# Inverse square roots by one power operation on GpSimd in place of an integer seed on VectorE and twelve Newton operations on GpSimd

## What is computed

```python
h = _layernorm(x) * (1 + ca) + sa              # root of a variance per token: "new.stats"
x = x + ga * attn_ref(h, guides)               # norms of token differences:   "new.dots"
h = _layernorm(x) * (1 + cb) + sb              #                               "new.again"
x = x + gb * ffn_ref(h, ...)                   # two layers of:
    q = l2norm(q) * qs;  k = l2norm(k) * ksc   # 8 heads, norms of q and k:    "proj.rsqrt"
    x = x + local_attention(rotary(q), rotary(k), v) @ wo
    h = (h - mu) / sqrt(var + 1e-05) * lg + lb #                               "ff.stats"
    x = x + (a * gelu(g)) @ w2 + b2
```

## Time and profile before

| | kernel before |
|---|---|
| median of three runs | 1008.69 us (1006.82 to 1008.88) |
| profiled execution: span | 1004.1 us |
| PE busy | 786.4 us (78%) |
| DVE busy | 698.4 us (70%), 1659 instructions |
| ACT busy | 652.1 us (65%) |
| POOL busy | 545.9 us (54%), 1116 instructions |

### The profile page before, as it was taken

How to read it: one execution, slowest core, us unless ns; L and a number is a source line. 1 busy time by engine, 2 the same in 40 slices (tenths; PEclk the granted TensorE clock), 3 DMA queues, 4 the chain that set the end, 5 groups by cost and what they waited for, 6 DMA issues and landing times.

```text
span 1004.1 us, 21260 instructions
## 1 busy us (share of the span) xinstructions
PE 786.4 (78%) x7119; PEld 556.9 (55%) x7151; DVE 698.4 (70%) x1659; ACT 652.1 (65%) x1539; POOL 545.9 (54%) x1116
## 2 busy tenths in 40 slices
PE   3344678797979797797979788898879787979974
PEld 3223456565656575565656565565656565656642
DVE  4466586494997794485897796494998765676742
ACT  1133474686876694686867685686786766867752
POOL 3146472373876481383786483373876563474601
PEclk9657699999999898999999999999999999999996
DMA  6000000000000000000000000000000000000000
GB/s 198 0 1 0 11 1 12 1 2 1 2 2 2 23 2 25 1 2 2 2 1 2 22 3 22 1 1 2 1 2 1 12 2 11 2 2 1 3 7 15
DMA packets 12298, 10.05 MB, mean 10 GB/s; under 512 B 1040, under 2 KB 11288, under 8 KB 12184
## 3 DMA queue, kind: packets, MB, share of 16 engines
q1 hardware_dynamic: 12184, 8.64, 2.8%
HBM read 6.54 MB, written 2.10 MB: 9 GB/s over the span
## 4 chain that ended last, share of the span: by engine, by line
PE 37%; DVE 21%; ACT 16%; issue 15%; POOL 9%; DMA 1%; POOLq 0%; SPq 0%; ACTq 0%; DVEq 0%
ACT probs L738 7%; PE pair L463 6%; PE dense L600 4%; DVE space L1176 3%; DVE q_norm L1179 3%; PE mixed L494 3%; PE dense L563 3%; POOL h_lo L1263 3%; PE dense L564 3%; PE dense L565 2%; PE dense L678 2%; PE pair L526 2%; DVE space L1174 2%; POOL qk L1288 2%; ACT squares L856 2%
## 5 line engine op out<-in xcount | busy, mean ns | idle before, releaser
L1288 POOL TENSOR_TENSOR qk<-space 128x512 f32<-128x512 f32 x128 | 197.3, 1554 | 28.6 <-DVE q_norm L1179 23.9
L738 ACT ACTIVATE probs<-pair,neg_max 128x128 f32<-128x128 f32 x512 | 138.5, 386 | 19.8 <-DVE neg_max L992 19.5
L1176 DVE TENSOR_TENSOR space<-dense,tables 128x512 f32<-128x512 f32 x128 | 87.3, 682 | 44.0 <-ACT space L860 44.0
L678 PE MATMUL dense<-wq_hi,h_hi 128*128 128x512 f32 x192 | 92.8, 483 | 21.5 <-DVE space L1176 12.2
L1285 POOL TENSOR_TENSOR space<-space,tables 128x512 f32<-128x512 f32 x64 | 84.2, 1316 | 30.9 <-ACT space L860 30.9
L856 ACT ACTIVATE squares<-dense 128x512 f32<-128x512 f32 x128 | 77.4, 605 | 34.0 <-PE dense L680 33.0
L463 PE MATMUL pair<-eye_s,probs 128*128 128x128 f32 x512 | 78.4, 286 | 26.0 <-ACT probs L738 26.0
L992 DVE TENSOR_REDUCE neg_max<-pair 128x4 f32<-128x512 f32 x128 | 82.1, 683 | 17.8 <-PE pair L526 17.6
L1179 DVE TENSOR_REDUCE q_norm<-squares 128x8 f32<-128x512 f32 x128 | 86.4, 675 | 0.0
L1277 POOL TENSOR_TENSOR h_lo<-shifted,h_hi 128x512 fp32r<-128x512 f32 x16 | 20.3, 1266 | 121.2 <-DVE h_hi L1163 121.2
L463 PEld LDWEIGHTS pair<-eye_s,probs 128*128 128x128 f32 x512 | 58.7, 145 | 46.6 <-ACT probs L738 44.0
(11 more groups left out here) (175 smaller groups left out, 1966.1 us busy)
## 6 DMA issues: line engine op xcount, KB each, us to landing
x_in<-n_L_attn_embeddings_dram SPq DMA_DIRECT2D x8, 256.0 KB, 3.2
out_dram<-hn SPq DMA_DIRECT2D x8, 256.0 KB, 2.5
qk<-in_L_ffn_wqkv_dram SPq DMA_DIRECT2D x1, 1536.0 KB, 6.2
qk<-in_L_ffn_w_dram SPq DMA_DIRECT2D x1, 682.0 KB, 7.5
wo_s<-in_L_ffn_wo_dram SPq DMA_DIRECT2D x2, 256.0 KB
o_t<-in_L_wmod_dram SPq DMA_DIRECT2D x1, 384.0 KB, 3.4
probs<-const_rotary_dram SPq DMA_DIRECT2D x1, 256.0 KB, 3.7
band_s<-const_band_dram SPq DMA_DIRECT2D x1, 256.0 KB, 7.8
```

The costliest lines, as they stand in the source:

```text
L678: pe.matmul(to[:, :], h_hi[:, rows], wq_hi[:, layer, cols], start=True, stop=False)
L738: last = act.activation(probs[:, ring, hh, :], banks[m][:, hh * P:(hh + 1) * P], ACT.Exp, bias=neg_max[:, ring, hh:hh + 1], scale=1.0)
L1176: dve.tensor_tensor(turned_s[:, t % 2, m, :].rearrange("p (h a b) -> p h a b", h=HEADS, a=2), halves[:, :, ::-1, :], rot(layer, t, 2 * m + 1),
L1288: pool.tensor_tensor(qk[s][:, t, m * INNER:(m + 1) * INNER], turned_c[:, t % 2, m, :], turned_s[:, t % 2, m, :], ALU.add).then_inc(added, 1)
```

## The change

DVE no longer halves the argument and no longer makes the seed; it writes `power`, which is the argument alone, and signals POOL. POOL raises it to -0.5 in one tensor_tensor with the operation `pow` against a tile `minus_half` that DVE filled with -0.5 at the start. The semaphores of the Newton steps and of DVE's wait on itself go, `root` is no longer written by DVE, and the first `proj.tile` of each pair gets a wait of DVE on `qk_powered`, its own last argument. The order of the steps on every engine stays as it is. The setup's own root of the guides keeps its integer seed and Newton steps on DVE.

```diff
-            def rsqrt_seed(root_, half_, ins_sem):
-                dve.tensor_scalar(root_.bitcast(I32), half_.bitcast(I32), -0.5, RSQRT_SEED, ALU.mult, ALU.add).then_inc(ins_sem, 1)
...
+            dve.memset(minus_half[:, :], -0.5).then_inc(halves_set, 1)
...
-                chain.done(dve.tensor_scalar(half_, mean_var_[:, :, 1], 1e-5, 0.5, ALU.add, ALU.mult))
-                rsqrt_seed(root_, half_, seeded)
+                dve.tensor_scalar(power_, mean_var_[:, :, 1], 1e-5, None, ALU.add).then_inc(powered, 1)
...
-                    own.done(dve.tensor_scalar(half_n[:, :], col[:, SS, :], 1e-30, 0.5, ALU.max, ALU.mult))
-                    rsqrt_seed(root_n[:, :], half_n[:, :], new_seeded)
+                    dve.tensor_scalar(power_n[:, :], col[:, SS, :], 1e-30, None, ALU.max).then_inc(new_powered, 1)
...
+                    if t % 2 == 0 and m == 0 and past(2 * before + t // 2):
+                        dve.wait_ge(qk_powered, 2 * before + t // 2)
                     dve.tensor_reduce(q_norm[:, 16 * (t % 2) + 8 * m:16 * (t % 2) + 8 * m + 8],
...
-                    dve.tensor_scalar(half[:, :], q_norm[:, :], 1e-24, 0.5, ALU.max, ALU.mult).then_inc(qk_self, 1)
-                    dve.wait_ge(qk_self, pair_ + 1)
-                    rsqrt_seed(root[:, :], half[:, :], qk_seeded)
+                    dve.tensor_scalar(power[:, :], q_norm[:, :], 1e-24, None, ALU.max).then_inc(qk_powered, 1)
...
-            def newton(root_, half_, scratch_, threes, base_sem, base, done_sem):
-
-                count = base
-                for k in range(3):
-                    for n, (to, a, b, op) in enumerate(((scratch_, root_, root_, ALU.mult), (scratch_, scratch_, half_, ALU.mult),
-                                                        (scratch_, threes, scratch_, ALU.subtract),
-                                                        (root_, root_, scratch_, ALU.mult))):
-                        ins = pool.tensor_tensor(to, a, b, op)
...
+            pool.wait_ge(halves_set, 1)
+
+            def inverse_root(to, of):
+
+                return pool.tensor_tensor(to, of, minus_half[:, 0:of.shape[-1]], ALU.pow)
 
             def unit_root(pair_):
 
-                pool.wait_ge(qk_seeded, pair_ + 1)
-                newton(root[:, :], half[:, :], scratch[:, :], three_halves[:, :], qk_newton, NEWTON * pair_, qk_rooted)
+                pool.wait_ge(qk_powered, pair_ + 1)
+                inverse_root(root[:, :], power[:, :]).then_inc(qk_rooted, 1)
```

More of the change, by code:

```diff
@@ L52 @@
 RSQRT_SEED = float(0x5F3759DF - (1 << 22))
-NEWTON = 11
 ROW_LN_G, ROW_LN_B, ROW_B2, ROW_B1 = 0, DEPTH, 2 * DEPTH, 3 * DEPTH
@@ L209, in adaln_block @@
         tables = sb("tables", [P, DEPTH, 2, 4, DH])
-        three_halves = sb("three_halves", [P, 32])
+        three_halves = sb("three_halves", [P, 2])
+        minus_half = sb("minus_half", [P, 32])
         columns = sb("columns", [P, N_ROWS])
@@ L259, in adaln_block @@
         mean_var = sb("mean_var", [P, TILES, 2])
-        half, root, scratch = sb("half", [P, 32]), sb("root", [P, 32]), sb("scratch", [P, 32])
-        half_f, root_f, scratch_f = sb("half_f", [P, 4]), sb("root_f", [P, 4]), sb("scratch_f", [P, 4])
+        power, root, scratch = sb("power", [P, 32]), sb("root", [P, 32]), sb("scratch", [P, 1])
+        power_f, root_f = sb("power_f", [P, 4]), sb("root_f", [P, 4])
         moments_f = sb("moments_f", [P, TILES, 6])
         mean_var_f = sb("mean_var_f", [P, TILES, 2])
-        half_n, root_n, scratch_n = sb("half_n", [P, 4]), sb("root_n", [P, 4]), sb("scratch_n", [P, 4])
+        power_n, root_n = sb("power_n", [P, 4]), sb("root_n", [P, 4])
         q_norm = sb("q_norm", [P, 32])
@@ L288, in adaln_block @@
         const_in, w_in, wo_in, rows_in, table_in = sem("const_in"), sem("w_in"), sem("wo_in"), sem("rows_in"), sem("table_in")
-        rows_cleared, setup_self = sem("rows_cleared"), sem("setup_self")
+        rows_cleared, setup_self, halves_set = sem("rows_cleared"), sem("setup_self"), sem("halves_set")
         setup_pe, setup_act, setup_dve, setup_pool = (
@@ L297, in adaln_block @@
         x_loaded, x_used, stored = [sem("x_loaded0"), sem("x_loaded1")], [sem("x_used0"), sem("x_used1")], sem("stored")
-        ff_shifted, ff_self, ff_seeded, ff_rooted = sem("ff_shifted"), sem("ff_self"), sem("ff_seeded"), sem("ff_rooted")
-        ff_newton, new_newton, qk_newton = sem("ff_newton"), sem("new_newton"), sem("qk_newton")
+        ff_shifted, ff_self, ff_powered, ff_rooted = sem("ff_shifted"), sem("ff_self"), sem("ff_powered"), sem("ff_rooted")
         ff_hi, ff_lo = sem("ff_hi"), sem("ff_lo")
-        new_self, new_seeded, new_rooted, new_normed = sem("new_self"), sem("new_seeded"), sem("new_rooted"), sem("new_normed")
+        new_self, new_powered, new_rooted, new_normed = sem("new_self"), sem("new_powered"), sem("new_rooted"), sem("new_normed")
         new_steps, new_squares, new_exp = sem("new_steps"), sem("new_squares"), sem("new_exp")
@@ L305, in adaln_block @@
         squared, summed, cosine_part, added = sem("squared"), sem("summed"), sem("cosine_part"), sem("added")
-        qk_self, qk_seeded, qk_rooted, qk_ready = sem("qk_self"), sem("qk_seeded"), sem("qk_rooted"), sem("qk_ready")
+        qk_powered, qk_rooted, qk_ready = sem("qk_powered"), sem("qk_rooted"), sem("qk_ready")
         final_scaled = sem("final_scaled")
@@ L911, in _ @@
             dve.memset(three_halves[:, :], 1.5)
+            dve.memset(minus_half[:, :], -0.5).then_inc(halves_set, 1)
             dve.wait_ge(const_in, 64)
-            g_half, g_root, g_tmp = half[0:GUIDES, 0:1], root[0:GUIDES, 0:1], scratch[0:GUIDES, 0:1]
+            g_half, g_root, g_tmp = power[0:GUIDES, 0:1], root[0:GUIDES, 0:1], scratch[0:GUIDES, 0:1]
             own.done(dve.tensor_tensor(gnorm, guides[:, :], guides[:, :], ALU.mult))
@@ L1007, in attention, with layer_stats @@
                             ALU.mult).then_inc(mix_normed, 1)
-            def layer_stats(src, moments_, mean_var_, half_, root_, chain, seeded):
+            def layer_stats(src, moments_, mean_var_, power_, chain, powered):
                 for j in range(TILES):
@@ L1030, in feed_forward @@
                     src = bank(i, slot, step)
-                    layer_stats(lambda j: src[:, j * P:(j + 1) * P], moments_f, mean_var_f, half_f[:, :], root_f[:, :],
-                                Chain(ff_self, 3 * before), ff_seeded)
+                    layer_stats(lambda j: src[:, j * P:(j + 1) * P], moments_f, mean_var_f, power_f[:, :],
+                                Chain(ff_self, 2 * before), ff_powered)
                 elif what == "norm":
@@ L1062, in feed_forward @@
                                              ALU.add).then_inc(empty(i, slot, step), 1)
-            NEW_SELF = 3 + 1 + 6 + 2 + 3 + 3
+            NEW_SELF = 2 + 6 + 2 + 3 + 2
             def new_unit(i, slot, step):
@@ L1073, in new_unit @@
                     dve.wait_ge(x_loaded[s], 16 * (unit + 1))
-                    layer_stats(lambda j: x_in[s][:, j, :], moments, mean_var, half_n[:, :], root_n[:, :],
-                                Chain(new_self, base), new_seeded)
+                    layer_stats(lambda j: x_in[s][:, j, :], moments, mean_var, power_n[:, :],
+                                Chain(new_self, base), new_powered)
                 elif what == "turn":
@@ L1085, in new_unit @@
                 elif what == "dots":
-                    own = Chain(new_self, base + 3)
                     dve.wait_ge(new_squares, before + 1)
-                    own.done(dve.tensor_scalar(half_n[:, :], col[:, SS, :], 1e-30, 0.5, ALU.max, ALU.mult))
-                    rsqrt_seed(root_n[:, :], half_n[:, :], new_seeded)
+                    dve.tensor_scalar(power_n[:, :], col[:, SS, :], 1e-30, None, ALU.max).then_inc(new_powered, 1)
                     for m in range(2):
@@ L1094, in new_unit @@
                 elif what == "sims":
-                    own = Chain(new_self, base + 4)
+                    own = Chain(new_self, base + 2)
                     dve.wait_ge(new_rooted, 3 * before + 2)
@@ L1106, in new_unit @@
                 elif what == "weights":
-                    own = Chain(new_self, base + 10)
+                    own = Chain(new_self, base + 8)
                     dve.wait_ge(new_exp, before + 1)
@@ L1122, in new_unit @@
                 elif what == "gate":
-                    own = Chain(new_self, base + 12)
+                    own = Chain(new_self, base + 10)
                     for m in range(2):
@@ L1145, in new_unit @@
                 elif what == "again":
-                    layer_stats(lambda j: x_in[s][:, j, :], moments, mean_var, half_n[:, :], root_n[:, :],
-                                Chain(new_self, base + 15), new_seeded)
+                    layer_stats(lambda j: x_in[s][:, j, :], moments, mean_var, power_n[:, :],
+                                Chain(new_self, base + 13), new_powered)
                 elif what == "stream":
```

(10 more changed lines are left out.)

## The result

The changed kernel takes 1002.2 us (median of 7 runs, 999.8 to 1006.0) against 1008.9 us before (7 runs, 1003.9 to 1011.6): ratio 0.994, 95% interval 0.992 to 0.997. The forecast was 978 us. The direction was right, the size not: 6 to 7 us came where 30 were expected.

The account below looks back on a forecast made before the run. Order of work and waits, not one engine's load, set the time. Gains of 17.6 + 4.9 + 3.6 + 2.6 + 1.5 = 30.2 us take the span from 1004.1 to 973.9, the median to 978 us (953 to 989, chance 0.60).

Parts of the forecast that it names:

- Slot 1 to slot 2: PE's 1.63 us wait for h_lo goes, as POOL wins 2.1 us and DVE 1.2; three places, 4.9 us.
- the last slot with attention: No gain or loss counted; the q and k scaling at 495.86 was given 2.4 us of slack for its root.
- Slots 2 and 3: DVE loses wide seeds (3.6 and 2.6 us) and the narrow seed and stall around new.sims (1.5 us).
- The exposed roots: DVE's waits for POOL's narrow roots where the pipeline fills and at the very end shrink, with six seeds: 17.6 us.
- The power's price: POOL's power at 46 ns for a column: 0.37 us on 4 columns, 1.66 us on 32.
- my own case: Power's cost per column on POOL: 46 ns chosen, at most 100 ns (0.6 us narrow, 3.4 us wide).
- Rival 3: Power so dear that roots come later than the series, deciding from 6.2 us wide; slower, 1050 us at 300 ns; chance 0.13.
- rival 4: Wide power near 5 us, narrow near 0.8, gains and losses even: 1007 to 1010 us; chance 0.05.
- The lock: On the shared SBUF port, a DVE instruction of the seed's kind waits for POOL's running instruction; seed 1.19 and 1.23 us.
- rival 2: Each wide power blocks DVE 1.4 us more, 17 us in slots 2 and 3: 995 us; chance 0.22 together with rival 1.
- newly loaded code: First call of newly loaded code on POOL takes some 6 us by the skill; the sum would be 984.

Follow-up runs that it names:

- f2: Changed kernel plus one wait: in slots with new activations, POOL's product of projection tile 0 waits for DVE's xn; 992.4 us, ratio 0.984.
- f1: Changed kernel with a cheap product for every power (roots all 0.25), POOL's products of tiles 0 and 2 waiting for DVE's xn and weights; 975.3 us, ratio 0.968.
- e3: Changed kernel with the wide power taken of only 8 of the 32 columns, the others held constant; 992.5 us, ratio 0.988.
- e1: Changed kernel with the 32-column roots by seed and Newton steps again, the 4-column roots still by power; 999.8 us, ratio 0.996.
- f3: Changed kernel with wide roots by Newton again, narrow ones by power, and POOL's product of tile 0 waiting for xn; 987.0 us, ratio 0.980.
- f4: Changed kernel with wide roots by Newton again, POOL's product of tile 0 waiting for xn and that of tile 2 for DVE's weights; 984.6 us, ratio 0.977.
- f6: Changed kernel with POOL's product of tile 0 waiting for xn, and DVE's seeds put back as dummies on a spare tile; 1003.7 us, ratio 0.996.
- e4: Changed kernel with a cheap product of the constant tile with itself in place of every power; 1003.8 us, ratio 0.998.

## Why the prediction was wrong, by its own steps

**Where the missing 24 us are.** The forecast had 30.2 us, the spans show 6.1. Slot 1 to slot 2 was to win 4.9 us and lost 3.3; the last slot with attention stood at nothing and lost 3.9. These 12 us are the wide power's price. Slots 2 and 3 were to win 7.7 us and won 1.6; 3.0 of the difference are the collision in the first slot 2. The exposed roots are 2.5 us short, 1.4 of it by the same collision. The rest, some 3 us, are the one F to F of 24.4 us and small pieces.

**The power's price: wrong, and both ends of my own case too.** I took 46 ns for a column, at most 100; it is 158. The floor of twelve operations' arithmetic was no guide. For the narrow root that is 1.02 in place of 0.37 us, which costs little. For the wide one it is 5.43 in place of 1.66 us, so it is longer than what it replaced. Rival 3 named this, with its point of decision at 6.2 us; rival 4 guessed "near 5 us, narrow near 0.8", and its 1007 to 1010 us are nearer to 1002 than my 978 is.

**The exposed roots: right.** Forecast 17.6 us; measured 13.1 by the first F and 2.0 at the end, 15.1. With the gate (f2) it is 14.5 and 2.4, and with free roots and both gates (f1) 19.0 and 3.2. The wait ahead of the first `xn`, 3.37 us, is now 1.20, that of the last `hn`, 3.36 us, 1.12:

```profile
20.09 1.11 DVE L993 TENSOR_SCALAR xn<-x_in,mean_var,root_n 128x128 f32<-128x128 f32 x4 [1.20 <-POOL root_n L1206]
...
977.15 1.36 DVE L993 TENSOR_SCALAR hn<-dense,mean_var_f,root_f 128x128 f32<-128x128 f32 x4 [1.12 <-POOL root_f L1206]
```

**Slot 1 to slot 2: right mechanism, wrong sign by the price.** Forecast 1.63 us won three times; measured 1.1 lost three times. POOL and PE after:

```profile
479.80 5.44 POOL L1206 TENSOR_TENSOR root<-power,minus_half 128x32 f32<-128x32 f32 x1
485.20 1.30 POOL L1243 TENSOR_TENSOR space<-space,tables 128x512 f32<-128x512 f32 x1
...
494.86 1.26 POOL L1235 TENSOR_TENSOR h_lo<-shifted,h_hi 128x512 fp32r<-128x512 f32 x1
```
```profile
496.25 0.50 PE L654 MATMUL dense<-wq_hi,h_hi 128*128 128x512 f32 x1 [2.71 <-POOL h_lo L1235]
```

From the start of the wide root to `h_lo` it was 503.45 - 489.65 = 13.80 us and is 494.86 - 479.80 = 15.06; PE's wait is 2.71 in place of 1.63 us. In e3, where a wide root takes 1.64 us, all but exactly the 1.66 that I had assumed, the interval is 26.4 us, 1.4 shorter: the step held at its own price. The other half of the step, 1.2 us that DVE was to win without the seed ahead of `h_hi`, did not come: `h_hi`, 0.41 us before, now stood itself beside POOL's product of 490.98.

```profile
491.05 1.50 DVE L1132 CAST h_hi<-shifted 128x512 fp32r<-128x512 f32 x1
```

The seed's 1.23 us (0.18 alone) had been mostly a wait for POOL, and the next instruction of DVE inherited the wait.

**Nothing was counted in the last slot with attention: wrong.** I looked for the slack of the q and k scaling at 495.86, which had 2.4 us. The one at 943.65 in the last slot already waited 1.03 us for its root before, so it had none, and PE is behind it:

```profile
932.33 5.44 POOL L1206 TENSOR_TENSOR root<-power,minus_half 128x32 f32<-128x32 f32 x1
```
```profile
937.80 2.29 DVE L944 TENSOR_TENSOR qk<-qk,root 128x2048 f32<-128x2048 f32 x1 [3.89 <-POOL root L1206]
```

It cost 3.9 us; with the wide Newton series (e1, f3, f4) the slot is back at 50.4 to 50.5.

**DVE in slots 2 and 3: about right in sum, undone by a collision that I had not asked for.** The forecast for the seeds and the stall was 1.5 us in a slot 2 and about 1.2 in a slot 3. Where nothing collides, f1 gives 0.9 to 1.1 and 0.9 to 1.4 against before, and the seeds that f6 puts back cost less than forecast in a slot 2 and more in a slot 3. In the changed kernel the first slot 2 lost 2.7 us: `xn` at 270.79 took 4.25 us with POOL's product and additions beside it from 271.12 on. This is the step that failed in kind and not in size. I asked of each stretch what DVE gains when it loses an instruction, and not what POOL does next when it is free sooner. In the changed kernel itself the collision is small (3.0 us in that slot, where the granted clock was 0.89 and in f2 0.96, and 1.4 by the first F), because the long wide power is a spacer too. With a power at the price that I had assumed it is larger: e3, whose wide root cost that, has a ratio of 0.988 where the forecast stands for 0.970, and its slots 2 and 3 are some 12 us longer in sum than f1's. How much of this the collision makes was not tried, since e3 was not run with the gates.

**The lock.** I wrote that a DVE instruction of this kind waits for POOL's running instruction, and rival 2 let it wait for a wide power. (At 519.06 POOL's operation was the product of 518.95, not an addition.) Half of it holds. POOL's product and addition stop DVE's steps, as above. The power does not: this `xn` lies wholly within a power that began at 558.08 and took 5.43 us.

```profile
561.11 1.10 DVE L993 TENSOR_SCALAR xn<-x_in,mean_var,root_n 128x128 f32<-128x128 f32 x4
```
```profile
558.08 5.43 POOL L1206 TENSOR_TENSOR root<-power,minus_half 128x32 f32<-128x32 f32 x1
```

So rival 2's 17 us did not come about. The Trainium skill, "SBUF — State Buffer", section "Who interferes with whom", has the shared pair held for a whole instruction: this agrees with POOL's products and additions and not with the power, whose operands are in SBUF as theirs are. It also says that who issues first decides; the rows agree in that a DVE step behind a product or addition lasts to its end. The 6 us that the prediction gives for newly loaded code do not show: the first power, at 19.04 us, took 1.02 us like the others.

**What is open.** The 1.5 us in one F to F (24.4 us) are TensorE's clock and no root: PE's 16 transposes of q and k took 3.30 us at 825.17, where they take 1.91 in f2 (at 820.76) and in before (at 835.10). The granted clock was half of full speed, 1.2 GHz, from 824.6 to 828.0 us, and full in the whole interval in f2 and in before. PE had waited 1.78 us ahead of it, but it had so in the other two as well; why the clock fell in this one stays open. Nor was it tried why the power leaves DVE alone, and no change keeps the wide power and takes away only the 3.9 us in the last slot.

## What to carry to other kernels

When a slow operation on an off-path engine becomes cheap, ask where its next operations will land, not only who waited for it: put the freed engine's long instructions on the neighbour's timeline, and where they meet short steps on the path, gate them with a wait on a semaphore that is there already. Here one such wait was worth as much as the change itself (0.994 to 0.984; by the spans 6.6 us against 6.1). And price an operation that no row shows by a run of its own width, or give the cases in which it is as dear as what it replaces more than the 0.18 that I gave them: a fixed price for each column can turn one instruction into the longest of its engine, so narrow roots may take the power while wide ones keep the series.

## What the runs showed of the hardware

A power on GpSimd costs 158 ns for each column of 128 rows on top of 0.38 us (1.02, 1.64 and 5.43 us for 4, 8 and 32 columns), where a product or addition of 32 columns takes 0.24 to 0.25 us. Within it VectorE's `xn` and its steps on 4 columns run at their own pace (1.10 us for four `xn`, 0.15 to 0.21 us for a step, in the changed kernel). Beside a GpSimd product or addition of 128x512 that began first, VectorE's tensor_scalar, tensor_tensor, scalar_tensor_tensor and copy on 4 columns in SBUF last to its end (0.17 becomes up to 1.25 us in e1, e3 and e4), and four `xn` go from 1.1 to 3.8 and 4.3 us. Not so for all that reads SBUF: its reciprocals on 4 columns (0.18 us), the statistics of `x_in` (0.28 us) and the reductions of `squares` (0.67 us) were as short beside GpSimd as alone. `hn`, which reads PSUM and writes 128x128, never took over 410 ns in before, after, e1, f2 or f3. A fall of TensorE's granted clock from 1.00 to 0.50 made 16 transposes last 3.30 in place of 1.91 us.
